# A decoder kernel on one core: each step holds four chunks of one sequence, with 512-column scores and values

## The chip, the cores and the metric

The kernel runs on one core of a Trainium2 chip, in one launch. The metric is the device time of that launch in microseconds (us); the kernel before was run three times. Everything is float32.

## The reference, cut to what matters

Two decoder layers work on `x`, 4 sequences of 1024 tokens with 256 numbers each. Each layer adds an attention, a cross-attention to a context of 77 rows, and a mixture of experts, with a layer norm behind each. The change lies in the first two parts of both layers.

```python
# layer 0: retention, 8 heads of 32, chunks of a sequence in order
attn = einsum('bhid,bhjd->bhij', qc, kc) * D
o_intra = einsum('bhij,bhje->bhie', attn, vc)
o_inter = einsum('bhid,bhde->bhie', qc * decay_q, S)
S_new = decay_s * S + einsum('bhjd,bhje->bhde', kc * decay_k, vc)
# layer 1: linear attention with running sums over the sequence
numerator = einsum('bsd,bsde->bse', sigma_q, cumsum(sigma_k v))
# both layers: cross-attention, 16 heads of 16, 77 context rows
attn = softmax(einsum('nqhd,nkhd->nhqk', q, k)); out = einsum('nhqk,nkhd->nqhd', attn, v)
# then: router, top 8 of 64 experts (layer 0) or 2 of 8 (layer 1)
```

## The kernel before, in words

A tile is 128 tokens. There are 32 tiles, and 8 steps (`STEPS`) of four tiles each. Before the change a step `i` holds tile `i` of each of the four sequences, so the four running states of layer 0's retention and of layer 1's linear attention are independent, and each moves by one tile a step.

The launch has four phases. `attention_phase` for layer 0 (retention, cross-attention, routing, scatter of the tokens to lists by expert); `feed_phase` (the 64 small experts and two shared experts); `attention_phase` for layer 1; `gated_phase` (8 large experts).

In `attention_phase` the order of the work of every engine is written out by hand: `SEQUENCE0` and `SEQUENCE1` (lines 208 to 224) are lists of jobs `(stage, ahead, part)`, and `steady` unrolls them, each job for step `n - ahead`. Every engine walks the same list and does its own side of each job, in order. TensorE (PE) fills a PSUM bank, and VectorE (DVE) or ScalarE (ACT) empties it. Most jobs take turns on four narrow banks; `ret`, `mx` and `sc` (`WIDE`, line 161) all use one place of four banks, so each has to wait until the one before is emptied.

The stages that matter here:
- `ret` (line 1057): scores of the retention, 16 matmuls with 32 contracted rows; DVE multiplies the result by a causal mask (line 788).
- `mix` (lines 1069, 1074): the state part and the value part of the retention into one bank. Each is 16 matmuls of 128 columns into quarters of 32 PSUM partitions; the state is laid out per head.
- `up` (line 1086 in layer 0, 1154 in layer 1): the sum that a tile adds to the state. In layer 0 DVE updates `total` (line 796) and spreads it, masked, into `state` (line 802), which the mix of the next step reads.
- `mx`, `mt` (lines 1186, 1192): the maximum of the scores per query and its transpose.
- `sc` (lines 1199, 1202): scores of one tile against the context, all 16 heads: 16 matmuls of keys and 16 that subtract the maximum, 128 columns each, on four row groups of 32. ACT takes the exponential of 77 x 2048 (line 663).
- `pv` (line 1212): the values, 16 matmuls of 128 columns; DVE transposes in 32 x 32 blocks, divides and transposes back (lines 859 to 871).
- `num` (lines 1144, 1147): numerator and denominator of layer 1's linear attention; it reads the state.
- `wo`, `wout`, `q`, `qk`, `v` are projections, `x1t`, `x2t`, `kt` transposes, `rt`, `top`, `rank` the routing, and `put` the scatter of the tokens to `lists` by indirect DMAs that GpSimd (POOL) issues: 32 a step in layer 0 (line 597), with a short `Rest` (line 158) between groups, and 8 a step in layer 1 (line 608).

A float32 matmul is two pairs of a weight load and a pass in the trace, so a job of 16 matmuls shows x32.

SP issues the loads and stores of whole steps, among them `xt` (line 468), `res_t` (line 504) and, for the shared experts, `sx` (line 98), each with four DMAs, one per sequence.

## Time and profile before

| | |
|---|---|
| three runs | 1983.88, 1987.17, 1990.72 us (median 1987.17) |
| span of the profiled execution | 1981.9 us |
| instructions | 45543, of them 17739 weight loads and 17739 passes on PE |
| PE / DVE / ACT / POOL busy | 1687.5 / 1165.2 / 623.2 / 892.7 us |
| mean granted TensorE clock | 0.922 |

The profiled execution gives its span, from the first to the last instruction; its whole time is not listed apart. The span lies 5.3 us under the median of the three runs, and that is taken for what lies around it.

How to read it: a group of instructions has its count behind an x. "busy" is the union of the group's instructions, "mean ns" the duration of one; matmuls overlap, so the mean is longer than the pitch. In a timeline the first two numbers are the start and the length of a merged piece, and a bracket holds the idle time of the engine before it and what ended it ("issue": nothing that the profile shows). PEclk 1.0 is the full TensorE clock, 0.5 the half.

### The profile page before, as it was taken

The page shows a single profiled execution, that of the slowest core. Times are in us where ns is not written, and L with a number is a line of the kernel's source. Part 1 is how long each engine was busy: PE and PEld are TensorE (multiplying, and loading weights), DVE is VectorE, ACT ScalarE, POOL GpSimd, SP SyncE. Part 2 cuts the span into 40 slices and gives each one's busy share as a digit, 9 for nine tenths or more (in the row PEclk, how much of TensorE's full clock was granted, in tenths as well). Part 3 has the DMA queues.
Part 4 walks back from the last instruction along what each step waited for, and adds up shares of the span by engine and source line. Part 5 has one row for each costly group of instructions (what it writes and reads, how often), then busy time and mean ns, then how long its engine had stood idle before and what let it go on. Part 6 is the DMA issues. An engine that isn't in the chain of part 4 may idle for free.

```text
span 1981.9 us, 45543 instructions
## 1 busy us (share of the span) xinstructions
PE 1687.5 (85%) x17739; PEld 1329.8 (67%) x17739; DVE 1165.2 (59%) x3228; ACT 623.2 (31%) x957; POOL 892.7 (45%) x1000
## 2 busy tenths in 40 slices
PE   6788888887689889998998478889977599999994
PEld 4566665666566567666676355667666499999994
DVE  4576655665432177776656456788765245655564
ACT  1232322222231277454555223445432111111110
POOL 0017556655758102888888856333323102222223
PEclk9999989998689999999998779999987699999997
DMA  9416543555448899888998922113111512333332
GB/s 325 150 46 199 184 150 116 190 169 191 146 147 237 219 304 295 285 278 273 297 294 290 317 78 82 57 65 121 69 39 65 164 49 76 91 94 98 98 94 69
DMA packets 269634, 322.61 MB, mean 163 GB/s; under 512 B 25083, under 2 KB 245487, under 8 KB 268655
## 3 DMA queue, kind: packets, MB, share of 16 engines
q1 hardware_dynamic: 234559, 226.38, 36.1%
q0 software_dynamic: 33024, 92.32, 14.4%
q8 instruction: 144, 2.36, 0.5%
q10 hardware_dynamic: 1840, 1.00, 0.2%
q14 instruction: 67, 0.55, 0.1%
HBM read 157.22 MB, written 162.40 MB: 161 GB/s over the span
## 4 chain that ended last, share of the span: by engine, by line
PE 68%; DVE 10%; issue 6%; DMA 6%; ACT 4%; POOL 3%; another core or an unknown queue 2%; SPq 1%; DVEq 1%; POOLq 0%; ACTq 0%
PE wide L2067 13%; PE d_yp L2079 6%; PE wide L110 4%; PE wide L127 4%; PE wide L1199 4%; PE wide L1202 3%; PE wide L1728 3%; PE e_yp L1739 3%; PE wide L1186 3%; PE bank L1033 3%; PE bank L1212 3%; PE bank L1219 2%; PE e_xp L1716 2%; PE bank L1105 2%
## 5 line engine op out<-in xcount | busy, mean ns | idle before, releaser
L1441 POOL DMA_INDIRECT big<-results,slots x256 | 263.4, 1029 | 202.1 <-DMA results<-e_y 125.5
L2067 PE MATMUL wide<-d_xt,d_ws 128*128 128x128 f32 x2272 | 279.0, 277 | 0.6 <-issue 0.6
L2067 PEld LDWEIGHTS wide<-d_xt,d_ws 128*128 128x128 f32 x2272 | 272.7, 193 | 4.5 <-issue 1.0
L597 POOL DMA_INDIRECT lists<-big,slots x160 | 159.6, 997 | 116.7 <-DVE slots L961 70.3
L663 ACT ACTIVATE pt<-wide 77x2048 f32<-77x2048 f32 x64 | 119.8, 1871 | 196.5 <-PE wide L1202 118.7
L1936 POOL DMA_INDIRECT d_picked<-results,slots x64 | 64.0, 1001 | 182.0 <-DMA results<-d_y 168.7
L1967 ACT ACTIVATE d_gate<-wide 128x512 f32<-128x512 f32 x71 | 42.4, 597 | 323.9 <-PE wide L2067 323.9
L2079 PE MATMUL d_yp<-d_wd,d_h 128*128 x568 | 134.2, 379 | 0.0
L1456 DVE SCALAR_TENSOR_TENSOR big<-big,weights 128x256 f32<-128x256 f32 x256 | 108.9, 487 | 41.6 <-DMA big<-results,slots 28.2
L110 PE MATMUL wide<-shared_sx,shared_sw 128*128 128x512 f32 x256 | 126.3, 616 | 7.7 <-DMA shared_sx<-res_t 5.2
L127 PEld LDWEIGHTS wide<-shared_sw,shared_sh 128*128 128x128 f32 x512 | 97.3, 191 | 45.1 <-issue 29.6
L127 PE MATMUL wide<-shared_sw,shared_sh 128*128 128x256 f32 x512 | 121.4, 380 | 3.6 <-DVE big L1697 3.6
L158 POOL TENSOR_TENSOR rest_ones<-rest_ones 128x4 f32<-128x4 f32 x108 | 121.0, 1120 | 2.0
L554 POOL TENSOR_TENSOR rs<-mv,eps 128x4 f32<-128x4 f32 x32 | 6.4, 199 | 234.9 <-DVE mv L712 234.1
L1212 PE MATMUL bank<-pt,vals 77*32 77x128 f32 x2048 | 89.6, 293 | 25.3 <-issue 15.4
L2079 PEld LDWEIGHTS d_yp<-d_wd,d_h 128*128 128x128 f32 x568 | 102.6, 190 | 11.0
L1998 DVE COPY d_ws<-big 128x1024 f32 x142 | 92.3, 693 | 27.5 <-issue 26.4
L2016 DVE TENSOR_TENSOR d_h<-d_gate,wide 128x512 f32<-128x512 f32 x71 | 48.7, 686 | 97.7 <-PE wide L2067 97.7
L1587 ACT ACTIVATE e_xt<-e_xp 128x1024 f32<-128x1024 f32 x80 | 81.9, 1024 | 76.5 <-PE e_xp L1716 48.7
L1716 PE MATMUL e_xp<-e_ident,e_x 128*128 128x128 f32 x640 | 86.9, 280 | 15.8 <-DMA e_x<-lists 12.2
L1199 PE MATMUL wide<-x1t,keys 32*77 32x128 f32 x1024 | 69.7, 315 | 35.8 <-issue 13.6
L1728 PE MATMUL wide<-e_xt,e_w1s 128*64 128x128 f32 x1280 | 89.4, 283 | 12.5 <-DVE e_w1s L1633 11.0
(280 smaller groups left out, 3488.8 us busy)
## 6 DMA issues: line engine op xcount, KB each, us to landing
lists<-zero SPq DMA_DIRECT2D x20, 2048.0 KB, 14.6
e_x<-lists SPq DMA_DIRECT2D x80, 512.0 KB
results<-e_y SPq DMA_DIRECT2D x80, 512.0 KB
d_x<-lists SPq DMA_DIRECT2D x71, 128.0 KB
results<-d_y SPq DMA_DIRECT2D x71, 128.0 KB
e_w<-in_L_w SPq DMA_DIRECT2D x2, 4096.0 KB
shared_sw<-in_x_t SPq DMA_DIRECT2D x32, 128.0 KB
x<-in_x SPq DMA_DIRECT2D x8, 512.0 KB
```

Source lines behind the costliest of these rows:

```text
L110: ins = nc.tensor.matmul(sp_h, self.sw1[:, c, u * P:(u + 1) * P], self.sx[:, s % 2, c], start=c == 0, stop=c == KC - 1)
L127: ins = nc.tensor.matmul(sp_y[b // 2][:, b % 2 * DM:(b % 2 + 1) * DM], self.sh[:, n % 2, b * P:(b + 1) * P], self.sw2[:, u], start=u == 0 ...
L158: step(self.nc.gpsimd.tensor_tensor(self.ones[:, 1], self.ones[:, 0], self.ones[:, 0], ALU.pow))
L597: pool.indirect_dma_start(out=lists, out_offset=bass.IndirectOffsetOnAxis(ap=slots[:, b, i, k:k + 1], axis=0), in_=z2[i % 3][:, b, :], in_ ...
L663: empties(nc.scalar.activation(pt[0:CTX, p % 2].rearrange("k (j n) -> k j n", j=4), ps[0:CTX], ACT.Exp, scale=score_scale), job)
L1199: mm(out[0:CTX, r, n * P:(n + 1) * P], keys[quarter(r), p, c, h * CTX:(h + 1) * CTX], qt[quarter(r), c, toks(p)], start=True, stop=False, ...
L1212: ins = mm(out[quarter(r), at:at + P], vals[:, p, c * 8 + 2 * r + h], pt[0:CTX, p % 2, of:of + P], start=True, stop=True)
L1441: pool.indirect_dma_start(out=picked[:, c % NG, b, :], out_offset=None, in_=results[0:-(-PAGES_OF_STEP[s] // 4) * 4 * R0, :], in_offset=ba ...
L1716: ins = tr(xp[:, h, (a * KC + c) * P:(a * KC + c + 1) * P], x[:, j % NX, h, a, c * P:(c + 1) * P], ident[:])
L1728: ins = mm(hp[h * H0:(h + 1) * H0, a * R0:(a + 1) * R0], w1s[:, j % NW1, h, a, c], xt[:, j % 2, h, a, c], start=c == 0, stop=c == KC - 1)
L2067: ins = mm(out[T % 2][:, a * P:(a + 1) * P], ws[:, T % NW, n, c, a * P:(a + 1) * P], xt[:, T % 2, c], start=c == 0, stop=c == KC - 1)
L2079: ins = mm(yp[T % 2][:, 0:DM], h[:, T % 2, c * P:(c + 1) * P], wd_flat[:, bass.ds(e * (HC * DM) + c * DM, DM)], start=c == 0, stop=c == HC ...
```

## The change

`TS` (512 tokens) and `TILES` (2) become constants; a step now holds four consecutive tiles of one sequence, and steps 2b and 2b+1 are sequence b. So:
- Rows of a step are contiguous in DRAM (`rows_of_step`); `xt`, `res_t` and `sx` are moved with one DMA instead of four.
- `sc` and `pv` take all 512 tokens of the step for a quarter of the heads, instead of one tile for all heads: 8 and 4 matmuls of 512 columns, instead of 32 and 16 of 128. The same columns in all. `wout` waits for all four `pv` of its step.
- The state of four tiles in a row is a chain within the step. `up` stands before `sc` in both sequences, DVE does the chain (8 small operations in layer 0, up to 4 in layer 1), and `mix` and `num` wait for their own step's states.
- In `mix` the state part is one matmul with 128 x 128 weights (heads on the diagonal) per tile and group instead of four: 4 a job for 16.
- In layer 1 `sigk` is written twice side by side, so that `up` fills all 128 partitions.

Left out of the diff below are renamed slices, semaphore counts (64 becomes 16) and the same `rows_of_step` in the later phases.

```diff
     def load_rows(self, sp, src_t, s):
-        for b in range(NB):
-            at = b * SEQ + s * P
-            sp.dma_start(self.sx[:, s % 2, :, b * P:(b + 1) * P],
-                         src_t[:, at:at + P].rearrange("(c p) n -> p c n", p=P)).then_inc(self.sx_in[s % 2], 16)
+        sp.dma_start(self.sx[:, s % 2], src_t[:, s * TS:(s + 1) * TS].rearrange("(c p) n -> p c n", p=P))\
+            .then_inc(self.sx_in[s % 2], 16)
...
+def rows_of_step(dram, i):
+
+    return dram[i * TS:(i + 1) * TS, :].rearrange("(j p) n -> p j n", p=P)
...
-    ("sc", 1, 0), ("mix", 0, 0), ("top", 2, 0), ("ret", 0, 1), ("pv", 1, 0), ("sc", 1, 1), ("mix", 0, 1), ("up", 0, 0),
+    ("up", 0, 0), ("sc", 1, 0), ("mix", 0, 0), ("top", 2, 0), ("ret", 0, 1), ("pv", 1, 0), ("sc", 1, 1), ("mix", 0, 1),
...
-    ("kvt", 1, 0), ("mt", 3, 0), ("wo", 2, 0), ("wo", 2, 1), ("sc", 3, 0), ("ln2", 4, 0), ("num", 1, 0), ("num", 1, 1),
+    ("kvt", 1, 0), ("mt", 3, 0), ("wo", 2, 0), ("wo", 2, 1), ("up", 1, 0), ("sc", 3, 0), ("ln2", 4, 0), ("num", 1, 0), ("num", 1, 1),
...
-    ("up", 1, 0), ("sig", 0, 0), ("mx", 2, 2), ("lv", 0, 0), ("ct", 1, 0), ("tri", 0, 0), ("tri", 0, 1), ("mx", 2, 3),
+    ("sig", 0, 0), ("mx", 2, 2), ("lv", 0, 0), ("ct", 1, 0), ("tri", 0, 0), ("tri", 0, 1), ("mx", 2, 3),
...
-            total = sb("total", [P, NB, 2, RD])
+            total = sb("total", [P, TILES * NB + 1, 2, RD])
             state = sb("state", [P, NB, 2, 4, RD])
...
-            turned, ratio = sb2[:].rearrange("p a n -> p (a n)"), rest[:].rearrange("p b e -> p (b e)")
+            turned, ratio = sb2[:].rearrange("p a n -> p (a n)"), sb("ratio", [P, TS])
...
-            sigk = sb("sigk", [P, NB, MEM])
+            sigk = sb("sigk", [P, NB, 2, MEM])
...
-            state = sb("state", [P, 2, 2 * (MEM + 1)])
+            state = sb("state", [P, TILES * NB, 2 * (MEM + 1)])
...
                 if stage == "kvt":
                     ps = filled(act, job)
-                    nc.scalar.activation(sigk[:], ps[:, 0:NB * MEM].rearrange("p (b n) -> p b n", b=NB), ACT.Copy)
+                    nc.scalar.activation(sigk[:], ps[:, 0:NB * MEM].rearrange("p (b n) -> p b n", b=NB).unsqueeze(2)
+                                         .broadcast_to([P, NB, 2, MEM]), ACT.Copy)
...
                     ps = filled(act, job)
-                    empties(nc.scalar.activation(pt[0:CTX, p % 2].rearrange("k (j n) -> k j n", j=4), ps[0:CTX],
+                    empties(nc.scalar.activation(pt[0:CTX, p % 2].rearrange("k (r n) -> k r n", r=4), ps[0:CTX],
                                                  ACT.Exp, scale=score_scale), job)
...
-                nc.vector.memset(state[:], 0.0).then_inc(state_done, 1)
                 make(nc.vector.memset(total[:], 0.0))
...
                 if stage == "up" and first:
                     ps = filled(dve, job)
                     added = ps[:, 0:NB * 2 * RD].rearrange("p (b g n) -> p b g n", b=NB, g=2)
-                    dve.wait_ge(state_done, i + 1)
-                    for g in range(2):
-                        ins = nc.vector.scalar_tensor_tensor(out=total[:, :, g], in0=total[:, :, g],
-                                                             scalar=decay_s[:, g:g + 1], in1=added[:, :, g],
-                                                             op0=ALU.mult, op1=ALU.add)
+                    at = i % TILES * NB
+                    for b in range(NB):
+                        for g in range(2):
+                            ins = nc.vector.scalar_tensor_tensor(out=total[:, at + b + 1, g], in0=total[:, at + b, g],
+                                                                 scalar=decay_s[:, g:g + 1], in1=added[:, b, g],
+                                                                 op0=ALU.mult, op1=ALU.add)
+                        if b < NB - 1:
+                            step(ins)
                     empties(ins, job)
                     emptied(dve, job)
                     for g in range(2):
                         ins = nc.vector.tensor_tensor(
-                            state[:, :, g], total[:, :, g].unsqueeze(2).broadcast_to([P, NB, 4, RD]),
+                            state[:, :, g], total[:, at:at + NB, g].unsqueeze(2).broadcast_to([P, NB, 4, RD]),
                             state_mask[:, g].unsqueeze(1).broadcast_to([P, NB, 4, RD]), ALU.mult)
                     ins.then_inc(state_done, 1)
...
                 if stage == "up" and not first:
                     ps = filled(dve, job)
-                    if i:
-                        emptied(dve, ("up", i - 1, 0))
-                    empties(nc.vector.tensor_tensor(state[:, :, 0:MEM + 1], state[:, :, 0:MEM + 1],
-                                                    ps[:, 0:2 * (MEM + 1)].rearrange("p (b n) -> p b n", b=2),
-                                                    ALU.add), job)
+                    at, n = i % TILES * NB, min(NB, TILES * NB - 1 - i % TILES * NB)
+                    for b in range(n):
+                        ins = nc.vector.tensor_tensor(state[:, at + b + 1, 0:MEM + 1], state[:, at + b, 0:MEM + 1],
+                                                      ps[:, b * (MEM + 1):(b + 1) * (MEM + 1)], ALU.add)
+                        if b < n - 1:
+                            step(ins)
+                    empties(ins, job)
+                    emptied(dve, job)
...
-                    if i or p:
-                        dve.wait_ge(att_done, NB * i + p)
-                    for h in range(2):
-                        ins = nc.vector.tensor_tensor(
-                            ratio[:].rearrange("p (c t h e) -> p h c t e", c=KC, t=4, h=2)[:, h],
-                            turned[:].rearrange("p (c h t e) -> p h c t e", c=KC, h=2, t=4)[:, h, :, :, 0:XD],
-                            rden[:].rearrange("p (c h t) -> p h c t", c=KC, h=2)[:, h].unsqueeze(3)
-                            .broadcast_to([P, KC, 4, XD]), ALU.mult)
-                    step(ins)
-                    nc.vector.transpose(att_t[:, :, p * P:(p + 1) * P], ratio[:].rearrange("p (c n) -> p c n", c=KC))\
-                        .then_inc(att_done, 1)
+                    c, h = p // 2, p % 2
+                    if h == 0 and i + c:
+                        dve.wait_ge(att_done, KC * i + c)
+                    step(nc.vector.tensor_tensor(ratio[:].rearrange("p (t h e) -> p t h e", h=2, e=XD)[:, :, h],
+                                                 turned[:].rearrange("p (t e) -> p t e", e=2 * XD)[:, :, 0:XD],
+                                                 rden[:].unsqueeze(2).broadcast_to([P, XH, XD]), ALU.mult))
+                    if h:
+                        nc.vector.transpose(att_t[:, c], ratio[:]).then_inc(att_done, 1)
...
-            if first:
-                pe.wait_ge(state_done, 1)
-            else:
+            if not first:
                 pe.wait_ge(ready, READY)
...
-                            for r in range(4):
-                                mm(out[quarter(r), at:at + P], state[:, b, g, r], qk[:, g, toks(b)], start=True,
-                                   stop=False, skip_group_check=True)
+                            mm(out[:, at:at + P], state[:, b, g].rearrange("p r n -> p (r n)"), qk[:, g, toks(b)],
+                               start=True, stop=False, skip_group_check=True)
...
                 if stage == "num":
-                    if i:
-                        emptied(pe, ("up", i - 1, 0))
-                    emptied(pe, ("kvt", i, 0))
                     for h in range(2):
                         emptied(pe, ("tri", i, h))
-                    wide_n = 2 * (MEM + 1)
+                    emptied(pe, ("up", i, 0))
+                    wide_n, at = 2 * (MEM + 1), i % TILES * NB
                     for b in range(2):
                         for h in range(2):
                             lanes = slice(h * MEM, (h + 1) * MEM)
-                            mm(outs[h][:, b * wide_n:(b + 1) * wide_n], sig[lanes, 0, b], state[lanes, b], start=True,
+                            mm(outs[h][:, b * wide_n:(b + 1) * wide_n], sig[lanes, 0, b],
+                               state[lanes, at + 2 * b + h], start=True,
                                stop=False, skip_group_check=True)
...
                 if stage == "up" and not first:
-                    for b in range(2):
-                        for h in range(2):
-                            ins = mm(out[h * MEM:(h + 1) * MEM, b * (MEM + 1):(b + 1) * (MEM + 1)],
-                                     sigk[:, 2 * b + h], v[:, 2 * b + h], start=True, stop=True)
+                    emptied(pe, ("kvt", i, 0))
+                    for b in range(NB):
+                        ins = mm(out[:, b * (MEM + 1):(b + 1) * (MEM + 1)], sigk[:, b].rearrange("p h n -> p (h n)"),
+                                 v[:, b], start=True, stop=True)
...
-                                     keys[quarter(r), p, c], start=True, stop=True)
+                                     keys[quarter(r), i // TILES, c], start=True, stop=True)
...
                 if stage == "sc":
                     emptied(pe, ("mt", i, 0))
-                    for n in range(4):
-                        c, h = n // 2, n % 2
-                        for r in range(4):
-                            mm(out[0:CTX, r, n * P:(n + 1) * P], keys[quarter(r), p, c, h * CTX:(h + 1) * CTX],
-                               qt[quarter(r), c, toks(p)], start=True, stop=False, skip_group_check=True)
-                        for r in range(4):
-                            ins = mm(out[0:CTX, r, n * P:(n + 1) * P], sel[quarter(r), n], peak_t[quarter(r), toks(p)],
-                                     start=False, stop=True, skip_group_check=True)
+                    c, h = p // 2, p % 2
+                    for r in range(4):
+                        mm(out[0:CTX, r], keys[quarter(r), i // TILES, c, h * CTX:(h + 1) * CTX], qt[quarter(r), c],
+                           start=True, stop=False)
+                    for r in range(4):
+                        ins = mm(out[0:CTX, r], sel[quarter(r), p], peak_t[quarter(r)], start=False, stop=True)
                     fills(ins, job)
                 if stage == "pv":
                     emptied(pe, ("sc", i, p))
-                    for c in range(KC):
-                        for h in range(2):
-                            at = (c * 2 + h) * P
-                            for r in range(4):
-                                of = (r * 4 + c * 2 + h) * P
-                                ins = mm(out[quarter(r), at:at + P], vals[:, p, c * 8 + 2 * r + h],
-                                         pt[0:CTX, p % 2, of:of + P], start=True, stop=True)
+                    c, h = p // 2, p % 2
+                    for r in range(4):
+                        ins = mm(out[quarter(r)], vals[:, i // TILES, c * 8 + 2 * r + h],
+                                 pt[0:CTX, p % 2, r * TS:(r + 1) * TS], start=True, stop=True)
                     fills(ins, job)
                 if stage == "wout":
-                    pe.wait_ge(att_done, NB * i + 2 * p + 2)
+                    pe.wait_ge(att_done, KC * (i + 1))
                     for bb in range(2):
                         for c in range(KC):
```

## Rows read from the trace of the kernel before

**Rows 1.** The page: engines, and the chain that ended last by engine.

```profile
PE 1687.5 (85%) x17739; PEld 1329.8 (67%) x17739; DVE 1165.2 (59%) x3228; ACT 623.2 (31%) x957; POOL 892.7 (45%) x1000
...
PE 68%; DVE 10%; issue 6%; DMA 6%; ACT 4%; POOL 3%; another core or an unknown queue 2%; SPq 1%; DVEq 1%; POOLq 0%; ACTq 0%
```

**Rows 2.** Windows by phase: busy us (count) per engine, clock, DMA.

```profile
65.00:568.00 503.00, 412.82 (x6172) 314.28 (x6170) 299.26 (x746) 139.13 (x179) 255.47 (x292) 0.89 0.47 155
...
1190.00:1515.00 325.00, 286.52 (x4420) 214.49 (x4420) 241.35 (x773) 132.23 (x188) 123.52 (x151) 0.92 0.21 69
```

**Rows 3.** Chain of waits in order: starts of `wo` mark layer 0's steps.

```profile
94.98 3.65 PE bank L1093 x16
...
148.25 3.65 PE bank L1093 x16
...
215.81 3.65 PE bank L1093 x16
```

**Rows 4.** Windows: first `sc` to third `sc`, in step 2 and step 6.

```profile
123.50:139.10 15.60, 13.36 (x391) 11.81 (x390) 10.21 (x33) 5.35 (x5) 0.00 (x0) 0.89 0.04 12
383.00:408.70 25.70, 19.73 (x392) 14.96 (x392) 10.33 (x34) 5.24 (x5) 17.28 (x18) 0.80 0.24 85
```

**Rows 5.** Timeline of PE, layer 0, the step without indirect DMAs.

```profile
125.12 0.40 PE L1202 MATMUL wide<-shared_sh,sel 32*77 32x128 f32 x8
125.44 0.43 PE L1069 MATMUL bank<-shared_sw,state 128*32 128x128 f32 x8
125.69 0.40 PE L1074 MATMUL bank<-big,shared_sx 128*32 128x128 f32 x8
...
127.50 1.17 PE L1057 MATMUL wide<-shared_sw 32*128 32x128 f32 x32
128.61 1.08 PE L1212 MATMUL bank<-pt,vals 77*32 77x128 f32 x32
131.82 0.46 PE L1199 MATMUL wide<-x1t,keys 32*77 32x128 f32 x8 [2.13 <-DVE big L788]
```

**Rows 6.** The same stretch of PE in the later step.

```profile
383.06 0.46 PE L1199 MATMUL wide<-x1t,keys 32*77 32x128 f32 x8 [1.08 <-DVE big L788]
...
385.37 0.35 PE L1199 MATMUL wide<-x1t,keys 32*77 32x128 f32 x2 [0.30 <-issue]
...
393.02 2.11 PE L1057 MATMUL wide<-shared_sw 32*128 32x128 f32 x30 [0.65 <-issue]
395.06 1.94 PE L1212 MATMUL bank<-pt,vals 77*32 77x128 f32 x32
...
408.69 0.46 PE L1199 MATMUL wide<-x1t,keys 32*77 32x128 f32 x8
```

**Rows 7.** Timeline of DVE in that step.

```profile
380.72 2.29 DVE L788 TENSOR_TENSOR big<-wide,causal 128x2048 f32<-128x2048 f32 x1 [3.03 <-remote]
...
383.83 0.42 DVE L883 TENSOR_TENSOR lg<-lg,nmax 128x256 f32<-128x256 f32 x1
...
387.85 1.00 DVE L903 TENSOR_TENSOR counts<-counts,chosen 128x64 f32<-128x64 f32 x4
...
408.16 1.29 DVE L802 TENSOR_TENSOR state<-total,state_mask 128x512 f32<-128x512 f32 x2
```

**Rows 8.** Timeline of PE, layer 1, one steady step.

```profile
1371.29 0.49 PE L1144 MATMUL bank<-state,sig 64*128 64x130 f32 x4
...
1386.49 1.98 PE L1176 MATMUL bank<-x1t,wq 128*128 128x512 f32 x4
1388.41 1.29 PE L1212 MATMUL bank<-pt,vals 77*32 77x128 f32 x25
...
1391.85 3.20 PE L1176 MATMUL bank<-x1t,wq 128*128 128x512 f32 x4
```

**Rows 9.** Timeline of DVE, layer 1: residual sums behind `wo`.

```profile
1371.19 0.66 DVE L706 TENSOR_TENSOR x<-bank,x 128x512 f32<-128x512 f32 x1
```

**Rows 10.** Waits of PE in the feed phase.

```profile
PE wide L110 <- DMA shared_sx<-res_t: 5.2, 1, 5.2
```

67 lines of the change are left out of this document (30 added, 37 removed).

## The prediction

> **What bounds the kernel now.** I read the page first: PE is busy 85% of the span and is 68% of the chain that ended last, so PE's in-order stream sets the time; "issue", where nothing visible is waited for, is 6% [rows 1]. The windows by phase show where the change acts: layer 0's attention, 503 us with PE busy 413, and layer 1's, 325 us with PE busy 287 [rows 2]. The other two phases keep their arithmetic.
>
> Then I asked for the pitch of a step. In the chain, layer 0's `wo` jobs start at 94.98, 148.25 and 215.81: one step of 53.3 us, then one of 67.6 [rows 3]. The same jobs are in both. The windows from the first `sc` to the third tell why: 391 passes take 15.6 us in step 2 and 392 passes take 25.7 us in step 6. The difference beside them is POOL: no instruction in the first, 18 (mostly indirect DMAs of `put`) in the second; the granted clock is 0.89 against 0.80 [rows 4]. PE's timeline shows the form of the loss: in step 6 the stream breaks off inside a job, with two passes and then 0.30 us of "issue" [rows 6], and later jobs run at the half clock, `ret` in 2.11 us for 1.17 and `pv` in 1.94 for 1.08 [rows 5, 6]. So about 10 us of a step in layer 0 are lost where POOL issues indirect DMAs while PE wants many small instructions. I take it that PE is not given instructions fast enough there, and that the idle time then costs clock. Layer 1 shows the same at the `pv` job that meets its 8 puts: 3.4 us from 1388.41 to 1391.85 for a job of about 1.0, and the next `q` takes 3.20 us against 1.98 for the one before [rows 8].
>
> **512 columns by themselves.** An `sc` job has 64 passes of 128 columns, 8192 in all; it will have 16 of 512, again 8192. Now 8 passes in four quarters take 0.22 to 0.25 us [rows 5], about 0.22 ns a column; four full-array passes of 512 columns take 1.92 us, from 1386.49 to 1388.41 [rows 8], 0.94 ns a column. So the quarters already run four at once, and the new job stays near 8192 x 0.22 = 1.8 us. Likewise `pv`. The bounds: nothing gained if only the columns count, some 0.05 us a job gained if each group of passes has a fixed price; I take 0. The Trainium skill (TensorE: Matmul & The Clock Gate, Measured speedup vs the span model) gives 3.07 times for four row tiles of 512 columns, less than the four that this trace shows at 128; by it the job would take 8192 x 0.94 / 3.07 = 2.5 us, which is a rival below.
>
> What does fall is the count. Between the first and third `sc` of a layer 0 step there are two `sc`, two `mix`, one `ret`, one `pv`, one `up` and `rank`: `sc` goes from 64 passes to 16, `pv` from 32 to 8, `mix` from 64 to 40, with as many weight loads. The 392 passes become 392 - 96 - 24 - 48 = 224 for the same columns.
>
> **Layer 0, a step with puts, from the start of the first `sc`.** `sc` ends at 1.95. `mix` now waits for its own states. DVE ends the causal mask as `sc` starts, at 380.72 + 2.29 = 383.01, and the logits at +1.2, 383.83 + 0.42 [rows 7]; then it does the new chain. No row shows it; the nearest is a chain of four 64-column operations, 1.00 us, so 0.25 a link [rows 7]. Each link has two operations here, I take 0.35, so 1.4 (bounds 1.0 and 8 x 0.34 = 2.7). Then the spreading, 1.29 [rows 7], and 0.1 for waits: states at +4.0. PE is idle about 2.1 us. `up` on PE (64 passes of 32 columns in quarters, 2048 x 0.22 ns and its fill: 0.8 us) is moved ahead of `sc`, into the 1.08 us that PE waits for DVE's mask [rows 6]; if `kt`'s copies come late that cover is gone and the 0.8 is paid.
>
> `mix` alternates a full-array matmul and four column quarters. Its columns cost what they did, 8 groups of 0.22 = 1.75. The change of tile shape from row quarters to column quarters shows 0.32 us between the starts 125.12 and 125.44, instead of 0.22, and 0.25 for the first group after it [rows 5]: I take 0.15 a change, 7 in a job, 1.05 (bounds 0 and 0.3 x 8 = 2.4). So `mix` runs from 4.05 to 6.85, `ret` to 8.05, the mask on DVE (2.29) to 10.4 with PE covering 0.9 of it by `pv`, the second `sc` to 12.4, the second `mix` to 15.25, `rank` 1.3 (1280 columns at 0.94 ns): third `sc` at 16.55. DVE's `top`, queued behind the new chain, ends near +7.6, before the mask is wanted.
>
> Against 25.6 now, from 383.06 to 408.69 [rows 6], that is 9.1 us less, and against the 15.6 of a step without puts 1.0 more. I don't expect all 9.1: PE idles 2 us twice in that stretch, so I leave the half clock for one `ret` and one `pv`, 0.94 + 0.86 = 1.8 us [rows 5, 6], and 1.8 for stalls in `ret` and `mix`, which keep 32 and 40 small passes. Net 5.5 a step (bounds 0 and 9.1). Five steps have the full pattern: 27.5. The draining steps have part of it: 4. Three early steps without puts lose 1.3 each: -4. POOL does not become the bound: 32 indirect DMAs, some six rests and eight small operations at 17.28 / 18 = 0.96 us [rows 4] are 44 us, below a step of 61.
>
> **Layer 1, per step.** `num` now waits for DVE's chain behind both residual sums. The second sum starts at 1371.19 [rows 9] and with its statistics takes 1.7, to 1372.9; up to four chained additions at 0.27 end at 1374.0, while `num` now starts at 1371.29 [rows 8]: 2.7 later, some 0.7 of it given back where `up` stood (eight passes, where four of `num` take 0.49). Cost 2.0 (bounds 1 and 3.5; `rank` and the second `sc` are queued behind it). The gain is 2.4 at the starved `pv` and 1.2 at `q`, 3.6, of which I take 3.3, in six steps: 6 x 1.3 - 2 x 2.0 = 4.
>
> **The rest.** DVE's `pv` side loses two transposes a step, off the path. `wout` waits for all four `pv`; four jobs of PE stand between in layer 1's list and most of a step in layer 0's. ACT's doubled `sigk` lies beside `wo`. Loads become one DMA for four; PE waits 5.2 us once for `sx` [rows 10], of which I take 4. Elsewhere I cost these loads at nothing, since x is loaded a step ahead.
>
> **Sum.** 27.5 + 4 - 4 + 4 + 4 = 35.5, so a span of 1981.9 - 36 = 1946. The median of the runs is 5.3 us above this span, which I add for what lies around it: 1951.
>
> **Rivals.** (a) Full relief: the thinner stream never starves and the clock holds. Then layer 0 gives 5 x 9.1 + 8 - 3, layer 1 gives 6 x 1.6 - 4, and the loads 4: 60, 1927. For it: nothing breaks off in step 2 at all [rows 4, 5]. Against it: new idle stretches of 2 us. (b) Slower: the stalls come from POOL's DMAs themselves, whatever the number of PE's instructions, and the waits for the state decide. The place is PE before `mix` and `num`; the price is 2.5 x 8 in layer 0 (wait and changes of shape, less what the mask wait hid) plus 2.0 x 8 in layer 1, less 4: +32, 2019. It decides as soon as less than about a third of the starved time comes back. For it: DVE and ACT start late in the same places ("remote", 3.03 us [rows 7]), though their streams are thin. The Trainium skill (Runtime: NRT & Kernel Launch, Instruction fetch mechanics) says that fetch is mostly hidden behind the issue of instructions, which speaks for (b); the breaks inside jobs speak against it. (c) Four quarters of 512 columns overlap only 3.07 times: 0.7 more for `sc` and 0.35 for `pv`, 64 of each, +67 on the forecast, 2018. Against: columns are columns, and passes of 128 start four at a time. (d) Gains and new waits cancel: within 6 us of now.
>
> **How the numbers follow.** What a measurement can tell from no change is about 0.3%, 6 us. Forecast 0.58, (a) 0.16, (b) 0.15, (c) 0.03, (d) 0.08. Faster 0.74, same 0.08, slower 0.18. The predicted time is the forecast's, 1951. Its own range is 1930 to 1975; to hold 8 in 10 it reaches over (a) down to 1912 and over (d) up to 1998.
>
> **What would show it.** Right: the window from first to third `sc` in layer 0 shows about 224 passes in 18 to 20 us with POOL as busy as now; `pv` after layer 1's puts takes about 1 us; a wait of 1 to 3 us before `mix` and before `num`, released by DVE (`state`, L802, and the chain of `up`); the new `sc` 1.8 us long. Wrong: breaks inside `mix` or `ret` as long as now with that POOL load, or `sc` of 2.5 us, or steps held by POOL.

## The result, and the profile after

The changed kernel takes 2002.89 us (median of 12 runs, 1996.57 to 2013.01), the kernel before beside it 1990.16 (12 runs). The ratio is 1.0074, with a 95% interval of 1.0053 to 1.0095: slower by 0.7%, where 1951 us and a gain were forecast. The profiled execution has a span of 2004.5 us.

The page after, engines and the chain that ended last by engine, against [rows 1]:

```profile
PE 1696.4 (85%) x12747; PEld 1206.7 (60%) x12747; DVE 1163.1 (58%) x3199; ACT 625.3 (31%) x957; POOL 897.2 (45%) x1000
...
PE 60%; DVE 15%; DMA 7%; issue 5%; another core or an unknown queue 4%; ACT 4%; POOL 3%; SPq 1%; DVEq 1%; POOLq 0%; ACTq 0%
```

5000 passes less have not made PE less busy. PE's part of the chain fell from 68 to 60% while DVE's rose from 10 to 15 and "another core or an unknown queue" from 2 to 4.

Windows by phase, against [rows 2] (us, then busy us and count of PE, PEld, DVE, ACT and POOL, granted clock, DMA share, GB/s):

```profile
74.00:580.00 506.00, 413.92 (x3530) 243.75 (x3530) 301.36 (x740) 139.73 (x178) 255.09 (x291) 0.87 0.45 151
1216.00:1537.00 321.00, 275.49 (x2108) 150.81 (x2107) 232.73 (x738) 132.41 (x186) 123.34 (x150) 0.93 0.21 68
```

Layer 0 has lost 3 us and some clock (0.87 for 0.89), layer 1 has won 4. Taken from start to start of the same jobs the picture is sharper. The first `wo` of layer 0 comes 6.8 us later. From it to the last (seven steps) it was 446.6 us, now 470.9: 24.3 more. From there to the first shared unit it was 79.28, now 60.23: 19.0 less. In layer 1, from the first pass of `sc` that subtracts the maximum to the last, it was 312.7, now 307.1: 5.6 less (from the start of the first `sc` job to the start of the last it is 2.6 less). The other stretches add what brings the sum to the 22.6 between the two spans, 6.8 of it between the feed phase's last matmul and layer 1's first `sc`.

The window from a first to a third `sc` in a step with puts, against the second line of [rows 4]:

```profile
335.70:363.50 27.80, 21.55 (x163) 10.63 (x162) 10.56 (x36) 5.35 (x5) 13.04 (x14) 0.58 0.18 62
```

27.8 us for 25.7, at a clock of 0.58, and the two are not quite alike: the stretch of before holds the 64 passes of `up`, while `up` now stands ahead of `sc` and so outside (163 passes). PE's timeline of that stretch, with `up` ahead of it, against [rows 6] (start, us, engine, line, operation; in brackets idle time before and its releaser):

```profile
333.82 0.32 PE L1085 MATMUL bank<-shared_sx 128*32 128x32 f32 x13 [1.28 <-issue]
334.39 0.70 PE L1085 MATMUL bank<-shared_sx 128*32 128x32 f32 x50 [0.25 <-issue]
335.52 0.25 PE L1085 MATMUL bank<-shared_sx 128*32 128x32 f32 x1 [0.43 <-issue]
335.70 2.56 PE L1196 MATMUL wide<-x1t,keys 32*77 32x512 f32 x8
337.48 2.48 PE L1199 MATMUL wide<-shared_sh,sel 32*77 32x512 f32 x8
343.90 0.77 PE L1068 MATMUL bank<-shared_sw,state 128*128 128x128 f32 x2 [3.94 <-DVE state L804]
344.60 0.66 PE L1073 MATMUL bank<-big,shared_sx 128*32 128x128 f32 x8
...
349.12 2.09 PE L1057 MATMUL wide<-shared_sw 32*128 32x128 f32 x32
351.14 1.94 PE L1205 MATMUL bank<-pt,vals 77*32 77x512 f32 x8
355.39 2.00 PE L1196 MATMUL wide<-x1t,keys 32*77 32x512 f32 x8 [2.31 <-DVE big L787]
...
359.03 0.55 PE L1068 MATMUL bank<-shared_sw,state 128*128 128x128 f32 x2
359.51 0.43 PE L1073 MATMUL bank<-big,shared_sx 128*32 128x128 f32 x8
...
363.47 1.10 PE L1196 MATMUL wide<-x1t,keys 32*77 32x512 f32 x8
```

Three things are to be seen. First, nothing breaks off inside `mix`, `ret` or `pv` here, though jobs still run at the half clock; `up`, which keeps its 64 small passes, still breaks off twice. Second, `mix` alternates its two shapes as forecast: the second one takes 3.2 us from 359.03 on at full clock, and the first, behind 3.94 us of idle time, 5.2 at half. Third, that idle time is a wait for DVE's `state`.

Over the five full steps, from the third `wo` to the last, both kinds of idle time of PE can be added up from the trace (gaps over 0.15 us). What is put down to "issue" fell from 31.5 us in 63 places to 16.1 in 24. What is put down to DVE rose from 10.6 to 38.7. The granted clock went from 0.92 to 0.85, and the five steps from 336.8 to 359.5 us.

DVE, ACT and POOL at the same moment, against [rows 7]:

```profile
332.24 2.29 DVE L787 TENSOR_TENSOR big<-wide,causal 128x2048 f32<-128x2048 f32 x1 [3.69 <-remote]
...
335.50 0.42 DVE L885 TENSOR_TENSOR lg<-lg,nmax 128x256 f32<-128x256 f32 x1
340.65 1.73 DVE L796 SCALAR_TENSOR_TENSOR total<-total,decay_s,bank 128x32 f32<-128x32 f32 x8 [4.73 <-remote]
342.42 1.34 DVE L804 TENSOR_TENSOR state<-total,state_mask 128x512 f32<-128x512 f32 x2
```

```profile
332.97 0.60 ACT L616 ACTIVATE shared_sx<-bank 128x512 f32<-128x512 f32 x1 [4.52 <-remote]
...
340.81 1.87 ACT L663 ACTIVATE pt<-wide 77x2048 f32<-77x2048 f32 x1 [4.44 <-PE wide L1199]
```

```profile
338.79 0.96 POOL L596 DMA_INDIRECT lists<-z,slots  x1 [0.30 <-issue]
339.76 1.04 POOL L163 TENSOR_TENSOR rest_ones<-rest_ones 128x4 f32<-128x4 f32 x1
341.09 1.04 POOL L596 DMA_INDIRECT lists<-z,slots  x1 [0.29 <-POOL rest_ones L163]
```

PE had ended `up` at 335.77 and `sc` at 339.96. DVE had stood idle since 335.9, and its first `total` starts at 340.65; ACT's exponential starts at 340.81. Both come within 0.2 us of each other, 0.9 to 1.1 after the end of POOL's last indirect DMA of a group (339.75). The mask of `ret` starts late too, 2.46 us after `ret` ended at 329.78, but that is in the middle of a group. The trace also holds the times of the semaphore updates, the signals by which a waiting engine is released: `up`'s comes at 340.63, 4.86 us behind the end of its last pass, where in the step without puts (130.94) the same update follows by 0.02. From 229 to 516 us, four steps, 32 of the 143 updates of PE that can be told are late by more than 0.5 us, and some two thirds of these come 0.7 to 1.1 us behind the end of the last DMA of a group, whether the next group or 16 us of nothing follows. Before the first put none is late. The page calls such a releaser "remote". The ends of PE's rows are modelled, so a late update can be a late signal or a late last write; the trace doesn't part them. By the Trainium skill (Perfetto Trace Analysis, Tensor Engine Instruction (MATMUL, LD_WEIGHTS)) the update goes out when PSUM has acknowledged the last bytes, behind the reported end. The undisturbed 0.02 us agree with that, and the section has nothing that would make it 4.86. The kernel before has as many late updates in the same steps, 38 of 144 from 215 to 485 us, by up to 4.4 us; there many small instructions stood in PE's queue, and its idle time showed as "issue".

Layer 1 at the `pv` that meets its eight puts, against [rows 8], and two new waits of PE (total, times, longest):

```profile
1413.95 1.98 PE L1174 MATMUL bank<-x1t,wq 128*128 128x512 f32 x4
1415.86 1.06 PE L1205 MATMUL bank<-pt,vals 77*32 77x512 f32 x8
1416.86 1.98 PE L1174 MATMUL bank<-x1t,wq 128*128 128x512 f32 x4
```

```profile
PE bank L1141 <- DVE state L836: 7.1, 5, 1.6
PE bank L1212 <- DVE att_t L874: 3.6, 2, 3.4
```

### The profile page after: what moved, and what is told of

The parts are those of the page before. It is cut to its first block, busy times and chain, and to the rows that moved or that the text cites. A ratio compares the mean times of both kernels' runs of the same rounds, so it can differ in the third digit from the quotient of the medians.

```text
span 2004.5 us, 35452 instructions
## 1 busy us (share of the span) xinstructions
PE 1696.4 (85%) x12747; PEld 1206.7 (60%) x12747; DVE 1163.1 (58%) x3199; ACT 625.3 (31%) x957; POOL 897.2 (45%) x1000
## 4 chain that ended last, share of the span: by engine, by line
PE 60%; DVE 15%; DMA 7%; issue 5%; another core or an unknown queue 4%; ACT 4%; POOL 3%; SPq 1%; DVEq 1%; POOLq 0%; ACTq 0%
PE wide L2057 13%; PE d_yp L2069 6%; PE wide L110 4%; PE wide L127 3%; PE wide L1196 3%; PE wide L1184 3%; PE wide L1199 3%; PE bank L1212 2%; PE e_yp L1730 2%; PE wide L1719 2%; DMA e_x<-lists 2%; PE e_xp L1707 2%; PE bank L1205 2%; DVE big L787 2%
## 5 line engine op out<-in xcount | busy, mean ns | idle before, releaser
L1432 POOL DMA_INDIRECT big<-results,slots x256 | 268.7, 1050 | 204.7 <-DMA results<-e_y 128.1
L663 ACT ACTIVATE pt<-wide 77x2048 f32<-77x2048 f32 x64 | 119.8, 1871 | 182.4 <-PE wide L1199 168.4
L1578 ACT ACTIVATE e_y<-e_yp 128x1024 f32<-128x1024 f32 x80 | 81.9, 1024 | 50.3 <-PE e_yp L1730 35.7
L1730 PE MATMUL e_yp<-e_w2s,e_ht 64*128 64x256 f32 x640 | 94.2, 414 | 3.8 <-ACT e_y L1578 3.8
```

The source lines that it names most:

```text
L663: empties(nc.scalar.activation(pt[0:CTX, p % 2].rearrange("k (r n) -> k r n", r=4), ps[0:CTX], ACT.Exp, scale=score_scale), job)
L1432: pool.indirect_dma_start(out=picked[:, c % NG, b, :], out_offset=None, in_=results[0:-(-PAGES_OF_STEP[s] // 4) * 4 * R0, :], in_offset=ba ...
L1578: return nc.scalar.activation(out, in_, ACT.Copy)
L1730: ins = mm(yp[:, h, a * DM:(a + 1) * DM], ht[lanes, j % 2, a], w2s[lanes, j % NW2, a, 0:DM], start=True, stop=True)
```

## The experiments

The experiments ran in four groups, each on another chip, and none of the four was like that of the first measurement: the kernel before takes 1871 to 1873 us on each. So no effect of these sizes can be read from the times alone between the first measurement and these; each is given as its ratio to the kernel before on the same chip. The changed kernel as it is has 1.0271 (1.0214 to 1.0329) on one of them. Smaller effects are read from stretches of one profile each: two pairs of kernels with the same layer 0 agree in it within 0.1 us from the first `wo` to the last.

**Without the puts.**

```diff
-                    for k in range(at, at + 4):
-                        pool.indirect_dma_start(
...
+                    nc.gpsimd.memset(shared.rest.sink[:, 8 * i + part_no:8 * i + part_no + 1], 1.0).then_inc(scattered[i % 3], 64)
```

> The changed kernel without the indirect DMAs by which GpSimd scatters layer 0's rows (steps 0 to 6): in place of each group of four, one small memset on GpSimd that raises the same semaphore, so that seven eighths of the rows never reach the experts' lists and the output is wrong in them; the rest of the work is the same. Theory H (while GpSimd works through a group of indirect DMAs, TensorE's completion signals reach VectorE and ScalarE only about 0.9 us after the group's last one, and the change has put a trip TensorE to VectorE to TensorE into that stretch): the steps with puts, 72 us apart, fall to the 55 us of the steps without, 5 x 17 = 85, so about 1918 us, and no wait of VectorE or ScalarE for an unknown releaser is left in them. Rival N (the steps are long by the change's own instructions and chain, whatever GpSimd does): the loss against the kernel before stays, over 1960 us.

> The kernel before with the same omission (seven eighths of layer 0's rows are never scattered). Theory H: its steps fall from 67.3 to the 53.3 us of those without puts, 5 x 14 = 70, so about 1920 us, and the changed kernel without the puts is level with it (ratio 0.995 to 1.002) where with puts it is 0.7% behind. Rival N: the changed kernel without puts stays 0.7% or more behind this one.

Measured: the changed kernel without puts 1924.5 us, ratio 1.0290 (1.0245 to 1.0335); the kernel before without puts 1867.06, ratio 0.9985 (0.9962 to 1.0009). On this chip layer 0's puts cost nothing that can be measured, in the one or the other, and without them on both sides the change loses 3.1% (1924.5 to 1867.06). The chip shows no late update, so theory H, which is about these, is neither shown nor refuted for the first chip; what is shown is that the change is slower by its own doing where nothing is late.

**A Rest after every second indirect DMA.** The edit: `if k == at + 2: shared.rest(pool)` in the same loop.

> The changed kernel with a Rest (a small GpSimd operation that is waited for) after every second indirect DMA of layer 0's scatter, not only after every fourth. Theory H: no signal is held for more than about 3 us, where it was up to 5; the late starts of the mask, the state and the exponentials shrink by half, some 1 to 3 us in each of the five steps, so 1988 to 1998 us, though GpSimd itself is busy 8 x 1.9 = 15 us longer in a step. Rival D (what disturbs is the DMAs themselves, not the length of a group): the signals are late as before, and with the puts stretched over more of the step it is as slow or slower, 2003 to 2015 us.

1940.79 us, ratio 1.0378 (1.0326 to 1.0430). With no late signal on this chip, theory H could not be tried; all that shows is that longer work on POOL costs about 1%.

**`up` and both `kt` earlier.** The line of the table becomes `kt 0, kt 1, ret 0, up, mt, rt, sc 0, mix 0, ...`

> The changed kernel with the job up placed right behind ret of the step's first half and both kt in front of it, so that its signal, the total chain and the state products come one group of puts earlier, while TensorE has mt, rt and the first sc to do. Theory H: the wait of mix for the state, 3.9 us in each step with puts, goes, and the first total no longer starts 4.7 us late on the path: 5 x 3 to 4 = 15 to 20 us less, 1983 to 1990 us. Rival N2 (the mix is held by other work, the mask or the exponential, which is as late): 1998 to 2004 us with a new wait in place of the state's.

1929.5 us, ratio 1.0332 (1.0293 to 1.0370), for 1.0271 as it is: no gain. PE's waits in five steps:

```profile
PE wide L1196 <- DVE big L787: 12.3, 5, 2.7
...
PE bank L1068 <- DVE state L804: 1.8, 4, 0.5
```

The wait of `mix` for the state is all but gone, from 8.8 to 1.8 us, and the wait of the second `sc` for the mask has taken its place, from 7.0 to 12.3. The chain of `total` and `state`, 3 us of DVE's queue, stands ahead of `top` and of the second mask at either place. That is rival N2.

**The changed kernel as it is, and two new orders.**

> The changed kernel as it is. Chips differ: on the one where the last four kernels ran, the kernel before takes 1872 us (1990 where the change was first measured), no signal of TensorE comes late during GpSimd's DMAs, and the change without puts costs 2.9%. On such a chip: theory S (the change itself lengthens each step of layer 0 by 5.4 us, from rt to the next wo, and layer 1 by some 18 us in all) 1925 to 1940 us, ratio 1.029 to 1.036. On a chip like the first one: 1.005 to 1.010 again, with late signals in the trace. Rival X (the loss without puts comes from leaving the puts out): 1.01 or less on this chip too.

1922.53 us, ratio 1.0271 (1.0214 to 1.0329): a little under the range of theory S (1.029 to 1.036) and far over what rival X allows. The loss is there with the puts in place.

```diff
-    ("up", 0, 0), ("sc", 1, 0), ("mix", 0, 0), ("top", 2, 0), ("ret", 0, 1), ("pv", 1, 0), ("sc", 1, 1), ("mix", 0, 1),
-    ("rank", 2, 0), ("sc", 1, 2), ("pv", 1, 1), ("sc", 1, 3), ("pv", 1, 2), ("pv", 1, 3),
+    ("sc", 1, 0), ("ret", 0, 1), ("mix", 0, 0), ("pv", 1, 0), ("top", 2, 0), ("sc", 1, 1), ("mix", 0, 1),
+    ("sc", 1, 2), ("rank", 2, 0), ("pv", 1, 1), ("sc", 1, 3), ("pv", 1, 2), ("pv", 1, 3),
```

(with `up` behind `ret 0`, as in the run before)

> The changed kernel with another order in layer 0's table only: both kt, ret 0 and up, then sc 0, ret 1, mix 0, pv 0, sc 1, mix 1, sc 2, rank and the rest, and top behind ret 1 for VectorE. Theory S, with the one wide bank as the chain that sets a step's second half: ret 1 no longer stands behind the mix that waits for the state, its mask no longer behind the top chain, sc 2 no longer behind rank: 3 to 5 us in each of eight steps, 25 to 40 us less than the changed kernel as it is. Rival V (VectorE is the bound there and only passes its wait on, to pv or rank): less than 10 us.

1950.82 us, ratio 1.0418 (1.0392 to 1.0445): 1.5% slower than the changed kernel as it is, where neither theory had a loss. PE now waits 18.0 us in five steps for the exponential ahead of `ret`, and DVE stands idle ahead of the first `pv`:

```profile
DVE sb L864 <- PE bank L1205: 22.9, 5, 4.7
```

I read that as rival V at a higher price than it was given (`rank` comes later, and its work on DVE pushes `pv` and the next step's first sums); no run parts the two waits.

> The changed kernel with layer 1's up ahead of wo in the table, so that VectorE adds to the state before it does the norm sums of wo. Theory S: num no longer waits 4 us for the state behind two norm sums; 2 to 3 us in each of six steps, 12 to 18 us less than the changed kernel as it is. Rival N3 (up waits for the evacuation of kvt in its new place and wo comes later by as much): 0 to 4 us.

1918.74 us, ratio 1.0243 (1.0218 to 1.0268): 0.3% better, which the two intervals can't tell from no difference, for the 12 to 18 us that were expected. In its profile layer 1 from the first `sc` to the last takes 292.9 us for 304.1, 11 us less, but the stretch ahead of that is 11 us longer in the same profile: PE waited 10.3 us for the `keys` of layer 1's start, and 1.0 in the changed kernel as it is. Whether the order has a part in that stays open.

> Both new orders together. Theory S: the gains add, 37 to 55 us less than the changed kernel as it is, so level with the kernel before or up to 1% ahead where that takes 1872 us, and ahead by 2% or more on a chip like the first. Rivals V and N3: 10 us less at most.

1934.73 us, ratio 1.0331 (1.0307 to 1.0356): 12 us more than the changed kernel as it is, where 37 to 55 less were expected. The loss of the first order is most of it; layer 0 from the first `wo` to the last takes 424.9 us for 403.1.

**The parts of the change undone one by one.** In `mix`:

```diff
-                            mm(out[:, at:at + P], state[:, b, g].rearrange("p r n -> p (r n)"), qk[:, g, toks(b)],
-                               start=True, stop=False, skip_group_check=True)
+                            for r in range(4):
+                                mm(out[quarter(r), at:at + P], state[:, b, g, r], qk[:, g, toks(b)], start=True,
+                                   stop=False, skip_group_check=True)
```

> The changed kernel with the decayed states multiplied head by head again (four 32-row products of a quarter each in place of one block-diagonal product of 128 rows). On a chip like the last two: theory M (the block-diagonal product takes the whole array while the products beside it take quarters, so mix is 3.07 us where it was 1.76): 1.3 us in each of 16 mixes, 12 to 21 us less than the changed kernel as it is, 1901 to 1911 us where that takes 1922. Rival M2 (mix lies beside VectorE's work and only fills a wait): 0 to 5 us.

1914.16 us, ratio 1.0221 (1.0187 to 1.0254), an interval that overlaps with that of the changed kernel; the profiles tell more. Layer 0 from first to last `wo`: 393.5 us for 403.1, 1.4 a step. Half of what theory M gave; the rest of the shorter `mix` turned into a longer wait for the mask (10.5 us in five steps for 7.0).

> The changed kernel with layer 0's up at its old place, behind the second mix; mix then waits for the states of the step before and reads those, so the retention's output is wrong, and the operations are the same in number and size. Theory S (what costs is that the eight additions of total and the two products of state, 3.0 us on VectorE, now stand ahead of top and so of the second mask, and that mix waits 1.9 us for them): 3 to 5 us in each of eight steps, 24 to 40 us less than the changed kernel as it is. Rival M alone (mix's own length is the whole loss): 0 to 6 us.

1911.9 us, ratio 1.0213 (1.0177 to 1.0249). First to last `wo` 390.5 us: 1.8 a step, less than expected too, and with no wait for a state left.

> The changed kernel with both: up at its old place (mix reads the states of the step before, so the retention's output is wrong) and states head by head. Theories S and M together: layer 0 gets back all that the change cost it, the sixth wo after the first with data comes 327 us later as in the kernel before (after: 347; the one part alone 334, the other 338); 1898 to 1906 us in all, and what is left against the kernel before lies in layer 1 (some 18 us) and the feed phase (3 to 5). Rival R (the 512 columns or VectorE's longer chain cost the remaining 7 us of layer 0): 1906 to 1912 us.

1897.62 us, ratio 1.0130 (1.0095 to 1.0166). First to last `wo` 384.4 us, for 388.3 in the kernel before and 403.1 in the changed one. The two parts are the whole loss of layer 0's steps (9.6 and 12.6 us alone, 18.7 together, of a loss of 14.8), and with them undone the steps are no slower than before. Left are 1.3%: 10 us between layer 0's last `wo` and the first unit (60.4 for 50.2) and the loss of layer 1.

`sc` and `pv` in pieces of 128 columns on the new order of tokens:

```diff
-                    for r in range(4):
-                        mm(out[0:CTX, r], keys[quarter(r), i // TILES, c, h * CTX:(h + 1) * CTX], qt[quarter(r), c],
-                           start=True, stop=False)
+                    for n in range(NB):
+                        for r in range(4):
+                            mm(out[0:CTX, r, toks(n)], keys[quarter(r), i // TILES, c, h * CTX:(h + 1) * CTX],
+                               qt[quarter(r), c, toks(n)], start=True, stop=False, skip_group_check=True)
...
```

> The changed kernel with scores and values in pieces of 128 columns again, on the new order of tokens. Both theories: 512 columns are not where the time goes, within 4 us of the changed kernel as it is where no signal comes late. On a chip like the first, where many small instructions break off while GpSimd issues its DMAs: 10 to 25 us slower. Rival W (the wide form itself costs, since four quarters of 512 columns run less well side by side): 10 us or more faster.

1933.32 us, ratio 1.0323 (1.0288 to 1.0357), half a per cent more than with 512, where the theories had 4 us (0.2%) at most; the two intervals overlap. Layer 0 from first to last `wo` takes 409.7 us for 403.1. The wide form is no part of the loss.

**The kernel before, profiled on such a chip.**

> The kernel before as it is, for its profile on a chip like the last three. Theory C (the late signals belong to the chip of the first measurement, not to the kernel): steps of layer 0 of 53 to 56 us with puts, as without them, no break inside TensorE's jobs and no late signal, 1865 to 1880 us. Rival: breaks and late signals as on the first chip, hidden in the time by something else. If this chip is like the first one, 1980 to 2000 us with steps of 67 us.

1872.01 us, ratio 1.0009 (0.9986 to 1.0031). A step with puts (window of one step, columns as above) and PE's timeline in it, then the same of the changed kernel as it is:

```profile
317.40:371.90 54.50, 48.69 (x835) 38.51 (x831) 41.97 (x104) 18.89 (x25) 40.07 (x46) 1.00 0.58 190
```

```profile
293.88 0.46 PE L1199 MATMUL wide<-x1t,keys 32*77 32x128 f32 x8
...
295.79 0.42 PE L1069 MATMUL bank<-shared_sw,state 128*32 128x128 f32 x8
296.04 0.40 PE L1074 MATMUL bank<-big,shared_sx 128*32 128x128 f32 x8
...
297.86 1.17 PE L1057 MATMUL wide<-shared_sw 32*128 32x128 f32 x32
298.96 1.08 PE L1212 MATMUL bank<-pt,vals 77*32 77x128 f32 x32
302.49 0.46 PE L1199 MATMUL wide<-x1t,keys 32*77 32x128 f32 x8 [2.44 <-DVE big L788]
```

```profile
329.40:386.80 57.40, 50.78 (x497) 31.17 (x494) 42.28 (x104) 18.89 (x25) 40.55 (x45) 1.00 0.53 179
```

```profile
303.64 1.10 PE L1196 MATMUL wide<-x1t,keys 32*77 32x512 f32 x8
304.53 1.07 PE L1199 MATMUL wide<-shared_sh,sel 32*77 32x512 f32 x8
307.47 0.46 PE L1068 MATMUL bank<-shared_sw,state 128*128 128x128 f32 x2 [1.88 <-DVE state L804]
307.86 0.42 PE L1073 MATMUL bank<-big,shared_sx 128*32 128x128 f32 x8
308.21 0.49 PE L1068 MATMUL bank<-shared_sw,state 128*128 128x128 f32 x2
...
310.54 1.17 PE L1057 MATMUL wide<-shared_sw 32*128 32x128 f32 x32
...
314.12 1.10 PE L1196 MATMUL wide<-x1t,keys 32*77 32x512 f32 x8 [1.42 <-DVE big L787]
...
316.01 0.49 PE L1068 MATMUL bank<-shared_sw,state 128*128 128x128 f32 x2
...
320.39 1.10 PE L1196 MATMUL wide<-x1t,keys 32*77 32x512 f32 x8
```

54.5 us here, with POOL busy for 40, where [rows 3] had 67.6. Nothing breaks off. Of some 1200 updates of PE that can be told in a trace none comes more than 0.5 us late, in this one and in the trace of every other run on these four chips; in the five steps "issue" has 0.9 us of PE's idle time before and 0.2 after, and DVE 16.0 and 19.8. From the first to the third `sc` it is 14.5 us before, with `up` in it, and 16.75 after, without. `mix` takes 1.8 us before (295.79 to 297.6) and 3.07 after (307.47 to 310.54): the block-diagonal product takes 0.42 us where the four quarters took 0.22, and the group behind it 0.36 for 0.22. At the 0.94 ns a column of full-array passes [rows 8] the 256 columns of the block-diagonal product would take an estimated 0.24 us, so most of the price goes with the change between the two shapes. An `sc` job takes 1.9 us up to the start of the next job in both kernels (293.88 to 295.79 and 314.12 to 316.01). PE's waits for DVE in five steps, before and after:

```profile
PE wide L1199 <- DVE big L788: 12.0, 5, 2.4
```

```profile
PE bank L1068 <- DVE state L804: 8.8, 5, 1.9
PE wide L1196 <- DVE big L787: 7.0, 5, 1.4
```

**Versions meant to win.** With states head by head, in layer 1 `up` ahead of `wo` (the last also between its halves), and in layer 0:

```diff
+    ("sc", 1, 0), ("top", 2, 0), ("ret", 0, 1), ("pv", 1, 0), ("up", 0, 0), ("sc", 1, 1), ("rank", 2, 0),
+    ("sc", 1, 2), ("mix", 0, 0), ("pv", 1, 1), ("sc", 1, 3), ("mix", 0, 1), ("pv", 1, 2), ("pv", 1, 3),
```

> A version meant to beat the changed kernel: states head by head; in layer 0 up, VectorE's total and state behind ret 1 and its mask (into the time in which VectorE waits for rank), mix 0 behind sc 2 and mix 1 behind sc 3; in layer 1 up ahead of wo. Theories S and M: 2.6 us of mix and 3 to 5 us of waits in each of eight steps, and the 4 us that the other order of layer 1 gave: 45 to 60 us less than the changed kernel as it is, about level with the kernel before. Rival V (as with the other new order: the rank chain on VectorE comes later and the next wout waits for it): no gain or a loss.

1884.64 us, ratio 1.0072 (1.0046 to 1.0098): 2% better than the changed kernel, 38 us where 45 to 60 were expected. First to last `wo` is 378.9 us, 9 less than in the kernel before; layer 1 and the way to it keep it behind.

> The last version with layer 1's up between the two halves of wo, so that neither up waits for the evacuation of v (0.6 us in a step) nor num for the state: 2 to 5 us less than the last version, 1880 to 1883 us. Rival: num waits for the state again, 1885 to 1890 us.

1879.79 us, ratio 1.0044 (1.0022 to 1.0066). PE's waits in five steps of layer 0:

```profile
PE wide L1057 <- ACT pt L663: 10.0, 5, 2.0
...
PE wide L1197 <- DVE big L787: 2.5, 5, 1.1
```

The wait for a state is gone, and the wait for the mask is 2.5 us for 12.0 in the kernel before.

```diff
+    ("sc", 1, 0), ("ret", 0, 1), ("top", 2, 0), ("pv", 1, 0), ("up", 0, 0), ("sc", 1, 1), ("sc", 1, 2), ("pv", 1, 1),
+    ("rank", 2, 0), ("sc", 1, 3), ("mix", 0, 0), ("pv", 1, 2), ("mix", 0, 1), ("pv", 1, 3),
```

> The same with another order in layer 0: ret 1 and its mask ahead of top on VectorE, sc 2 behind sc 1 at once, pv 1 ahead of rank, both mixes late. Theory S (the mask of ret 1 behind top is what sets the second half of a step: sc 1 starts 2.2 us after TensorE could, and at half clock): 1 to 3 us in each of eight steps, 8 to 22 us less than the version beside it, so 1860 to 1875 us, ahead of the kernel before by up to 0.6%. Rival V (rank's chain on VectorE ends later and pushes pv, wo's sums and the next step): no gain, or up to 20 us more.

1888.89 us, ratio 1.0087 (1.0058 to 1.0115): rival V again. The steps are no shorter (382.8 us for 379.0 from first to last `wo`), and the end of layer 0, from the last `wo` to the first unit, takes 63.4 us for 57.4. No version beat the kernel before on these chips. On a chip like the first one none was run.

## Why the prediction was wrong

The terms against what the two profiles of the first chip show, in us, with the same differences on the other chips (the kernel before and the changed one as it is, one profile each):

```
                                     forecast   first chip   others
start to layer 0's last wo              -23.5        +31.1    +19.5
last wo to the first unit                -4          -19.0     +8.9
first unit to the end of the feed        -4           +7.7     -1.2
to layer 1's first sc                     0           +6.8     +9.4
first to last sc of layer 1              -4           -5.6    +16.9
the rest                                  0           +1.6     +2.8
sum                                     -35.5        +22.6    +56.3
```

Of the first row, 6.8 and 4.7 us come ahead of the first `wo`: at the start of layer 0 nothing covers the chain, and PE waits 3.2 us for `state` on both chips, which was costed at nothing. The rows of layer 1 count from the passes of `sc` that subtract the maximum; from job start to job start its two rows are +5.2 and -2.6 on the first chip and +8.8 and +16.8 on the others.

**The step that failed** is the relief of layer 0's full steps: "I take it that PE is not given instructions fast enough there", from which came 9.1 us less in the stretch from the first to the third `sc`, 5.5 taken, 27.5 in five steps. Measured the stretch was 27.8 us for 25.7, though `up` had left it, and the five steps took 22.7 us more. Half of what the forecast wanted back did come: "issue" fell by 15.4 us in the five steps. But PE's waits for DVE rose by 28.1, where on the other chips they rose by 3.8. What is late in those stretches is PE's completion signals, by up to 5 us, and with 5000 passes less they are no sooner (32 late ones in four steps, for 38). The thinner stream changes what is seen: mostly a break in PE before, more often a wait for DVE now. The forecast held that evidence, DVE's mask with 3.03 us from "remote" [rows 7], and gave it to a rival. And the change put a new trip from PE over DVE back to PE (`up`, `total`, `state`, `mix`) beside POOL's groups, where each signal on it can be held. That the lateness goes with those groups is read from the times of the updates in the traces of that chip, and from the steps without puts. No experiment showed it, since the chips of the experiments do not have it, and no run tells whether all of the 28.1 us is owed to it.

Three smaller terms were off beside it. The count of 224 passes still had `up` in it, which the same forecast moves out of the stretch: it is 163. The 16.55 us of the stretch without `up` were set against 25.6 and 15.6 with it, so 0.8 us of the gain was only moved. And the 5.3 us around the span came from other runs than the profiled one; the profiled run of the changed kernel took 2006.87 us with a span of 2004.5, so 2.4.

**Rival (b)**, slower because the waits for the state decide, is the way it went, short of its 2019 us. There was relief all the same. It can be seen by comparing what the change did on the first chip with what it did on the others, where it has nothing to relieve: on the first it came out 28 us better in the end of layer 0 (forecast 4), about 20 better in layer 1 (forecast 3.3 in six steps, 20), and 12 worse up to layer 0's last `wo`. So the relief lay less in the full steps, where a new trip crosses the late signals, than in the drain. There the kernel before took 79.3 us from the last `wo` to the first unit, and 50.2 on the other chips; its updates come up to 8.0 us late in that stretch, those of the changed kernel up to 1.7.

**What the change costs where nothing is disturbed** was right for the stretch: 16.55 us forecast, 16.75 measured on the other chips. Its parts: eight operations of `total` 1.73 us (forecast 1.4, upper bound 2.7), `state` 1.29 (1.29), PE idle ahead of `mix` 1.9 (2.1), `mix` 3.07 (2.8), DVE's `top` done at +7.7 (+7.6). But it was set against the 15.6 us of a step on the first chip. Elsewhere the kernel before needs 14.5, so the cost is 2.3 us in the stretch. `up`, taken as hidden behind a wait, takes 0.76 us ahead of it, and no wait stands there. In all a step takes 2.7 us more (55.6 to 58.3), not 1.0, and moving `up` forward only moved the wait on to the mask.

**512 columns** were costed at nothing, and that was right: `sc` takes 1.9 us in both forms, and undoing them brought nothing back. Sixteen passes of 512 columns at 0.48 us [rows 8] in 1.9 us are four at once. The Trainium skill (TensorE: Matmul & The Clock Gate, Measured speedup vs the span model) has 3.07 times for four row tiles of 512 columns, and by it an estimated job of 2.5 us. The trace does not agree, and rival (c) is out.

**Layer 1.** `pv` behind the puts takes 1.06 us for 3.4 and `q` 1.98, as forecast. `num` waits 1.4 us in a step for `state`. The 16 us that the waits were to cost in all meet the 16.9 of the other chips partly by luck: there PE waits 8.6 us for `state` in that stretch, its waits for the maxima grow from 13.4 to 18.4, and `up` ahead of `wo` gave 11 us back. Not seen was the start of layer 1, where nothing covers the chain either: `num` waits 3.2 us for `state` there, `up` 1.1 for the copy of `v`, and the clock is 0.68 for 0.72. `wout` waits for `att_t`, 3.6 us in layer 1 and 3.9 at the end of layer 0, which was costed at nothing. The wait for `sx` went from 5.2 to 2.4 us, 2.8 gained for 4, but from 2.0 to 3.7 on the other chips, so it is no sure gain. The work of the small experts, from its first matmul to its last, took some 3 us longer in the changed kernel on both chips (483.5 for 480.3, and 483.5 for 480.1); why stays open.

## What to carry to other kernels

When an engine looks starved beside heavy work of another, look first whether its consumers start late as well: then the signals may be late, fewer instructions are no sure help, and each new trip between engines in that stretch can cost one late signal more. A small chain on an in-order queue costs its whole length to whatever is queued behind it; put it where that engine is waiting anyway, as the two late versions did (24 us in layer 0's steps, of which the states head by head are 10). And profile on more than one chip before a stall is laid to the kernel.

## What was not expected of the hardware

The same kernel takes 1990 us on one chip and 1871 to 1873 on four others. The small experts' work and the last phase, each from its first matmul on, are alike on both (480 and 480 us, 439 and 438); the difference lies in the two attention phases and layer 0's drain, where POOL issues indirect DMAs (the puts, and in layer 1 gathers of the experts' results too). On the one chip, a step with puts takes 67 us and a step without 53, and updates of PE come up to 5 us late in the steps, most of them 0.7 to 1.1 us behind the end of a group of these DMAs. Late updates alone need not cost time: the feed phase has 60 of them on that chip, up to 3.6 us late, and the experts' work in it takes the same 480 us. On the others a step takes 54.5 to 57.6 us with puts and 54.1 to 55.6 without, though the DMAs have the same length (0.96 us) and spacing (0.30). What makes the one chip so stays open. The other surprise is the price of a full-array product of 128 columns among products of quarters: 0.42 us where four quarters took 0.22, and 0.14 more for the group that follows it, which made 3.07 us of a `mix` of 1.8.
